# A segment softmax over sorted edges: carries applied to whole rows, or to the ends of a partition only

## The reference, cut to what matters

```
alpha = leaky_relu(s_src[row] + s_dst[col], negative_slope=0.2)      # (200000, 4)
seg_max = segment_max(alpha, row)
m = maximum(seg_max, 0.0)
ex = exp(alpha - m[row])
seg_sum = segment_sum(ex, row)
deg = segment_sum(ones, row)
denom = seg_sum + (E - deg)[:, None] * exp(-m)
alpha_n = ex / denom[row]
out = segment_sum(alpha_n[:, :, None] * h[col], col)                 # then + bias, residual
```

## Time and profile before

| | |
|---|---|
| median of three runs | 5434.14 us |
| span of the profiled execution | 5435.2 us |
| instructions | 98,961 |
| busy: PE, DVE, ACT, POOL | 4092.1, 3597.3, 3044.1, 3260.0 us |
| mean granted TensorE clock | 0.905 of full speed |

### The profile page before, as it was taken

The page is one execution under the profiler, slowest core; times in us unless marked ns, Lnnn a source line. Parts: engine busy times, 40 slices in busy tenths (PEclk is TensorE's granted clock), DMA queues, the critical chain, the costliest instruction groups (busy, mean ns, idle before and its releaser), DMA issues. The chain is left out here.

```text
span 5435.2 us, 98961 instructions
## 1 busy us (share of the span) xinstructions
PE 4092.1 (75%) x22798; PEld 3403.2 (63%) x22799; DVE 3597.3 (66%) x8070; ACT 3044.1 (56%) x4591; POOL 3260.0 (60%) x3487
## 2 busy tenths in 40 slices
PE   5778777777777777700699987777777777777778
PEld 5766666666666666500699965666666666666666
DVE  8945444444444444429999986777777777777776
ACT  5555555555555455401677756666666666666665
POOL 2357777777777777740000005777777777777774
PEclk9988888888888888855899999999999999999999
DMA  8865555555555554495200036666656565666655
GB/s 312 325 198 149 140 141 137 138 140 141 140 137 140 141 140 138 149 88 16 58 0 0 0 94 170 146 144 147 146 145 146 144 147 144 147 144 147 146 145 135
DMA packets 1212202, 734.52 MB, mean 135 GB/s; under 512 B 929642, under 2 KB 1031204, under 8 KB 1205388
## 3 DMA queue, kind: packets, MB, share of 16 engines
q1 hardware_dynamic: 862700, 336.19, 30.8%
q0 software_dynamic: 131424, 275.52, 17.3%
q10 hardware_dynamic: 218048, 122.49, 7.6%
HBM read 562.32 MB, written 165.09 MB: 134 GB/s over the span
## 5 line engine op out<-in xcount | busy, mean ns | idle before, releaser
L1059 POOL DMA_INDIRECT g_q<-q_d,g_aux x1660 | 1573.0, 948 | 1407.4 <-DMA pw<-g_q 901.7
L577 POOL DMA_INDIRECT rec_d<-rec,place x1568 | 1542.1, 984 | 503.2 <-issue 475.9
L1366 PE MATMUL g_hp<-pw,g_mix 128*128 x3328 | 876.0, 386 | 305.9 <-ACT g_mix L1263 300.6
L690 PE MATMUL lk<-tab_sd,low 128*128 128x196 f32 x3136 | 1065.5, 427 | 0.0
L1377 PE MATMUL g_ap<-g_hid,g_oh 128*128 128x256 f32 x3328 | 881.0, 387 | 140.2 <-DVE agg L1169 135.4
L626 DVE TENSOR_REDUCE rank<-equal 128x4 f32<-128x512 bf16 x392 | 260.6, 684 | 1024.9 <-ACT equal L554 1012.8
L1283 ACT ACTIVATE g_hid<-g_q 128x512 f32<-128x512 f32 x832 | 524.0, 630 | 713.6 <-DVE g_q L1155 698.4
L1366 PEld LDWEIGHTS g_hp<-pw,g_mix 128*128 128x128 f32 x3328 | 616.1, 190 | 463.7 <-issue 388.2
L1155 DVE TENSOR_TENSOR g_q<-g_hp,g_q 128x512 f32<-128x512 f32 x832 | 573.6, 689 | 477.3 <-DMA g_q<-q_d,g_aux 353.7
L687 PE MATMUL lk<-mask,hx 122*128 122x245 bf16 x1568 | 482.9, 308 | 430.6 <-ACT low L543 430.6
L554 ACT ACTIVATE equal<-rk,minus_two 128x512 bf16<-128x512 f32 x392 | 259.5, 685 | 967.5 <-DMA rec_d<-rec,place 561.3
(11 more groups left out here) (231 smaller groups left out, 5064.4 us busy)
## 6 DMA issues: line engine op xcount, KB each, us to landing
low_row<-rows_d SPq DMA_DIRECT2D x392, 256.0 KB
rec_d<-pad ACTq DMA_DIRECT2D x49, 1152.0 KB, 4.2
g_ea<-rec_d SPq DMA_DIRECT2D x208, 256.0 KB, 4.4
rec<-in_ea ACTq DMA_DIRECT2D x196, 256.0 KB
hx_row<-rows_d SPq DMA_DIRECT2D x392, 98.0 KB
g_lrow<-low_row_d SPq DMA_DIRECT2D x208, 128.0 KB, 4.3
g_q<-q_d,g_aux POOLq DMA_INDIRECT x1660, 2.9
rec_d<-rec,place POOLq DMA_INDIRECT x1568
```

The source lines that it names most:

```text
L577: pool.indirect_dma_start(rec_d, bass.IndirectOffsetOnAxis(ap=place[0:n, at, j:j + 1], axis=0), rec[0:n, at, j, :], None).then_inc(s_sc[at ...
L690: mm = pe.matmul(to[:, NB:LK], low[:, par, 1, slots], tab_sd[:, :, :].rearrange("p h a -> p (h a)"), start=False, stop=True, skip_group_ch ...
L1059: pool.indirect_dma_start(qg[:, par, j, :], None, q_d, bass.IndirectOffsetOnAxis(ap=aux[:, par, j, F_IDX - F_LOW:REC - F_LOW].bitcast(I32) ...
L1366: mm = pe.matmul(hp[u][:, k * HID:(k + 1) * HID], mix[:, par, 2 * u + k, :], pw[:, bass.ds(b[k], 1), :].rearrange("p o f -> p (o f)"), sta ...
```

## The change

Pieces are no longer joined in every slot. The scores have only the maximum of their own piece subtracted (`al - sc` right after the first `spread`), and the exponentials and sums are those of the piece. What was exchanged across partitions is joined in small tiles (`whole`): `peak` and `piece` hold, for the row's last and its first piece and four heads, the piece's own value and that of the whole run. The sums of the end pieces are scaled by `fall` = exp(own maximum - whole maximum) before they are exchanged. At the end ScalarE takes logarithms: of the piece sums in every slot (`line`), and of own and whole sums in the small tile `piece`. The difference of the small logarithms, less the difference of the maxima, is added to `line` in the slots of the first run (with `from_first`) and of the last run (with `to_last`); `one_run` keeps it from being added twice where a row holds one run alone. The weight is exp(`al` - `line`), by ScalarE.

```
+piece = sb("piece", [P, 2, 2, HEADS], F32, ctx)
+peak = sb("peak", [P, 2, 2, HEADS], F32, ctx)
+fall = sb("fall", [P, 2, HEADS], F32, ctx)
+one_run = sb("one_run", [P, 1], F32, ctx)
+tiny = sb("tiny", [P, 1], F32, ctx)
...
         act.activation(high_dst[:, at], fld[:, at, DHIGH], ACT.Copy).then_inc(s_ld, 1)
     for h in range(HEADS):
         act.wait_ge(s_mr, h + 1)
+        act.activation(line[h], al[:, h, :], ACT.Exp)
+        act.activation(sc[:, h, :], sc[:, h, :], ACT.Exp, scale=-1.0).then_inc(s_exp, 1)
+    act.wait_ge(s_mr, HEADS + 1)
+    act.activation(fall[:, :, :], peak[:, 1, :, :], ACT.Exp).then_inc(s_exp, 1)
+    for h in range(HEADS):
+        act.wait_ge(s_dn, h + 1)
+        act.activation(line[h], sc[:, h, :], ACT.Ln, bias=tiny[:, 0:1]).then_inc(s_ln, 1)
+    act.wait_ge(s_dn, HEADS + 1)
+    act.activation(piece[:, :, :, :], piece[:, :, :, :], ACT.Ln, bias=tiny[:, 0:1]).then_inc(s_ln, 1)
+    for h in range(HEADS):
+        act.wait_ge(s_fin, h + 1)
         act.activation(al[:, h, :], al[:, h, :], ACT.Exp)
-        act.activation(sc[:, h, :], sc[:, h, :], ACT.Exp, scale=-1.0).then_inc(s_exp, 1)
-    for pair in ((0, 1), (2, 3)):
-        for h in pair:
-            act.wait_ge(s_dn, h + 1)
-            act.activation(line[h], sc[:, h, :], ACT.Ln).then_inc(s_ln, 1)
-        for h in pair:
-            act.wait_ge(s_ln, h + 1)
-            act.activation(line[h], line[h], ACT.Exp, scale=-1.0).then_inc(s_r0, 1)
 @block.vector
 def _(v):
     link = Chain(v, s_ch)
+    v.memset(tiny[:, :], 1e-30)
     v.memset(fwd[:, S:S + 1], 0.0)
     v.memset(flagT[:, :, :], 0.0)
     v.memset(carT[:, :, :], 0.0).then_inc(s_e0, 1)
...
-    def carried(k, outs, op, both):
+    def carried(k, both):
...
-        for o, h in zip(outs, range(HEADS)):
-            ins = v.scalar_tensor_tensor(out=o, in0=from_first[:, :], scalar=car[:, 0, h:h + 1], in1=o,
-                                         op0=ALU.mult, op1=op)
-        link(ins)
-
-    def later(h, o, op):
-        return v.scalar_tensor_tensor(out=o, in0=to_last[:, :], scalar=car[:, 1, h:h + 1], in1=o, op0=ALU.mult, op1=op)
+    def whole(to, own, op):
+        v.scalar_tensor_tensor(out=to[:, 0, :], in0=car[:, 0, :], scalar=from_first[:, S - 1:S], in1=own[:, 0, :],
+                               op0=ALU.mult, op1=op)
+        link(v.scalar_tensor_tensor(out=to[:, 1, :], in0=car[:, 0, :], scalar=from_first[:, 0:1], in1=own[:, 1, :],
+                                    op0=ALU.mult, op1=op))
+        v.tensor_tensor(to[:, 0, :], to[:, 0, :], car[:, 1, :], op)
+        link(v.scalar_tensor_tensor(out=to[:, 1, :], in0=car[:, 1, :], scalar=to_last[:, 0:1], in1=to[:, 1, :],
+                                    op0=ALU.mult, op1=op))
...
+    v.tensor_scalar(one_run[:, :], from_first[:, S - 1:S], -1.0, 1.0, ALU.mult, ALU.add)
+    carried(0, False)
+    for h in range(HEADS):
+        ins = v.scalar_tensor_tensor(out=al[:, h, :], in0=from_first[:, :], scalar=car[:, 0, h:h + 1], in1=al[:, h, :],
+                                     op0=ALU.mult, op1=ALU.add)
+    link(ins)
...
-    def spread():
...
+    def spread(h):
+        return v.tensor_tensor_scan(sc[:, h, ::-1], next_no_head[:, ::-1], hd[:, ::-1, h], 0.0, ALU.mult, ALU.max)
+    for h in range(HEADS):
+        ins = spread(h)
+    link(ins)
+    v.tensor_copy(peak[:, 0, 0, :], hd[:, S - 1, 0:HEADS])
+    link(v.tensor_copy(peak[:, 0, 1, :], sc[:, :, 0]))
+    v.tensor_copy(ends[:, :, :], peak[:, 0, :, :]).then_inc(s_endr, 1)
     link(v.tensor_copy(low_in[:, :], fld[:, :, LOW]))
+    v.wait_ge(s_ld, CH)
+    for h in range(HEADS):
+        v.tensor_tensor(al[:, h, :], al[:, h, :], sc[:, h, :], ALU.subtract).then_inc(s_mr, 1)
+    link(v.tensor_scalar(low_out[:, :], low_in[:, :], BLK - 1, None, ALU.bitwise_and))
     exchange(1, ALU.max, True)
-    link(v.tensor_scalar(low_out[:, :], low_in[:, :], BLK - 1, None, ALU.bitwise_and))
-    carried(1, [sc[:, h, :] for h in range(HEADS)], ALU.max, True)
-    for h in range(HEADS):
-        link(later(h, sc[:, h, :], ALU.max))
-        v.tensor_tensor(al[:, h, :], al[:, h, :], sc[:, h, :], ALU.subtract).then_inc(s_mr, 1)
     v.tensor_copy(lowrow[:, :], low_out[:, :]).then_inc(s_lr, 1)
+    carried(1, True)
+    whole(peak[:, 1, :, :], peak[:, 0, :, :], ALU.max)
+    v.tensor_tensor(peak[:, 1, :, :], peak[:, 0, :, :], peak[:, 1, :, :], ALU.subtract).then_inc(s_mr, 1)
...
-        link(v.tensor_tensor(sc[:, h, :], sc[:, h, :], al[:, h, :], ALU.add))
+        link(v.tensor_tensor(sc[:, h, :], sc[:, h, :], line[h], ALU.add))
...
-    spread()
+    for h in range(HEADS):
+        spread(h).then_inc(s_dn, 1)
+    v.wait_ge(s_dn, HEADS)
+    v.tensor_copy(piece[:, 0, 0, :], hd[:, S - 1, 0:HEADS])
+    link(v.tensor_copy(piece[:, 0, 1, :], sc[:, :, 0]))
+    v.wait_ge(s_exp, HEADS + 1)
+    link(v.tensor_tensor(piece[:, 1, :, :], piece[:, 0, :, :], fall[:, :, :], ALU.mult))
+    v.tensor_copy(ends[:, :, :], piece[:, 1, :, :]).then_inc(s_endr, 1)
     exchange(2, ALU.add, True)
-    carried(2, [sc[:, h, :] for h in range(HEADS)], ALU.add, True)
+    carried(2, True)
+    whole(piece[:, 1, :, :], piece[:, 1, :, :], ALU.add)
+    v.engine_nop().then_inc(s_dn, 1)
+    v.wait_ge(s_ln, HEADS + 1)
+    link(v.tensor_tensor(piece[:, 0, :, :], piece[:, 1, :, :], piece[:, 0, :, :], ALU.subtract))
+    link(v.tensor_tensor(piece[:, 0, :, :], piece[:, 0, :, :], peak[:, 1, :, :], ALU.subtract))
+    link(v.tensor_scalar(piece[:, 0, 0, :], piece[:, 0, 0, :], one_run[:, 0:1], None, ALU.mult))
     for h in range(HEADS):
-        later(h, sc[:, h, :], ALU.add).then_inc(s_dn, 1)
-    v.wait_ge(s_ld, CH)
-    for h in range(HEADS):
-        v.wait_ge(s_r0, h + 1)
-        v.wait_ge(s_dn, h + 1)
-        link(v.tensor_tensor(line[HEADS], sc[:, h, :], line[h], ALU.mult))
-        link(v.scalar_tensor_tensor(out=sc[:, h, :], in0=line[HEADS], scalar=2.0, in1=line[h],
-                                    op0=ALU.subtract, op1=ALU.mult))
-        link(v.scalar_tensor_tensor(out=al[:, h, :], in0=al[:, h, :], scalar=-1.0, in1=sc[:, h, :],
-                                    op0=ALU.mult, op1=ALU.mult))
+        link(v.scalar_tensor_tensor(out=line[h], in0=from_first[:, :], scalar=piece[:, 0, 1, h:h + 1], in1=line[h],
+                                    op0=ALU.mult, op1=ALU.add))
+        link(v.scalar_tensor_tensor(out=line[h], in0=to_last[:, :], scalar=piece[:, 0, 0, h:h + 1], in1=line[h],
+                                    op0=ALU.mult, op1=ALU.add))
+        v.tensor_tensor(al[:, h, :], al[:, h, :], line[h], ALU.subtract).then_inc(s_fin, 1)
```

More of the change, by code:

```diff
@@ L745, in build @@
                 s_mr, s_exp = sem("max_taken"), sem("exp_ready")
-                s_dn, s_ln, s_r0 = sem("denominator_ready"), sem("log_ready"), sem("first_reciprocal_ready")
+                s_dn, s_ln, s_fin = sem("sums_spread"), sem("log_ready"), sem("log_weight_ready")
                 s_lr, s_ls, s_ld = sem("lowrow_ready"), sem("lowrow_stored"), sem("dst_digits_ready")
@@ L883, in _ @@
                     link(v.memset(to_last[:, S - 1:S], 1.0))
-                    rows = [al[:, h, :] for h in range(HEADS)]
-                    carried(0, rows, ALU.add, False)
+                    v.tensor_scalar(one_run[:, :], from_first[:, S - 1:S], -1.0, 1.0, ALU.mult, ALU.add)
[4 more added lines that the diff above has]
+                    link(ins)
                     for k in range(CH):
@@ L920, in _ @@
                         link(v.tensor_tensor(sc[:, h, :], sc[:, h, :], rest[:, :], ALU.mult))
-                        link(v.tensor_tensor(sc[:, h, :], sc[:, h, :], al[:, h, :], ALU.add))
+                        link(v.tensor_tensor(sc[:, h, :], sc[:, h, :], line[h], ALU.add))
                         ins = v.tensor_tensor_scan(hd[:, :, h], no_head, sc[:, h, :], 0.0, ALU.mult, ALU.add)
                     link(ins)
-                    spread()
-                    exchange(2, ALU.add, True)
```

## The result

The changed kernel takes 5405.74 us, the median of four runs (5404.22 to 5406.91), against 5434.32 us for the kernel before (four runs, 5433.72 to 5435.36): 28.6 us less, a ratio of 0.995 with a 95% interval of 0.9938 to 0.9962. The forecast was 5407.3 us and 26.8 us less.

What follows compares the result with a forecast made beforehand. VectorE was taken to bound the softmax stage: 54.58 us removed less 27.8 added gives 26.8, so 5434.14 - 26.8 = 5407.3 us. The stated range was 5404.5 to 5412.0, with the forecast given 0.89.

Steps and rivals of the forecast that it cites:

- The path: Softmax stage: VectorE alone sets its end, busy 125.2 of 128.5 us; a gain there reaches the kernel's end whole.
- the signs: Expected in the profile: second `spread` about 14.5 us earlier, last loop near 2576.4, weigh loop near 2601.8 at its old pace.
- What was removed: VectorE's softmax stage: sixteen long joins, the 0.89 us wait for reciprocals and twelve last-loop instructions, together 54.58 us.
- every microsecond off VectorE moves the barrier by one: Softmax stage, 2499.51 to 2627.98 us: VectorE time saved moves the barrier equally, as long as ScalarE does not become last.
- What was added: Softmax stage: new last loop 23.16, final exponential 1.63, small instructions 2.6 and round trip 0.4, together 27.8 us.
- The last loop: VectorE's end of the softmax stage: two linked instructions and one subtraction per head, 23.16 us, so no gain by itself.
- The tail: After VectorE's last subtraction: 0.04 us for ScalarE to notice and 1.59 for one exponential, 1.63 us.
- The round trip for the small logarithm: Before the last loop: VectorE waits for ScalarE's logarithm of 16 columns, 0.4 us, cheap end 0.2, dear end 1.0.
- The small instructions: Sixteen added on VectorE, ten linked at 0.20 and six at 0.08 or 0.10: 2.6 us, between 1.3 and 5.4.
- rival 1: End of softmax stage: ScalarE sets the end, four exponentials piling up behind VectorE, 6.0 us more, 5413.3; chance 0.05.
- rival 2: Weigh loop or gather stage: the gain is given back and the time stays near 5434; chance 0.03.
- rival 3: Loop bodies: moved code makes a loop fetch its body each turn, slower, 5716 at the dear side; chance 0.02.

Runs made afterwards that it cites:

- experiment 2: Kernel before without the sixteen joins over 1664 slots, 1 added in the logarithm: first spread scan to weigh loop 103.80 us, 25.2 less; median 5407.76 us.
- experiment 1: Changed kernel run again unaltered, twice: median 5411.69 us against 5436.55 for the kernel before, and on another chip 5401.31 against 5430.26.
- experiment 3: Kernel before with only the last step changed to exponentials of a difference of logarithms, long joins kept: median 5421.59 us against 5436.55.
- experiment 10: Kernel before with eight small memsets added to VectorE's program where it waits for a DMA: median 5430.96 us against 5430.26.
- experiment 4: Changed kernel without the eight long additions of the last loop: first spread scan to weigh loop 86.29 us, 15.9 less than changed; median 5394.02 us.
- experiments 7 and 8: Changed kernel with GpSimd subtracting `line` from `al`: median 5413.98 us; with GpSimd also multiplying by `rest`: 5419.12 us; kernel before 5435.71.

## Why the prediction was right

**The path.** The prediction held that VectorE's work sets the length of the stage, and that a microsecond at the barrier is worth a microsecond at the end. Both hold: the stretch fell by 26.84 us and the weigh loop kept its 578.53 us, to 0.02, in every kernel here. Counted from the first scan, the signs came where they were forecast: second `spread` 14.51 us earlier (14.5), last loop from 2572.07, which is 2576.58 on the clock of the kernel before (2576.4), weigh loop at 2601.69 (2601.8). The gather stage moves by 3.6 us, with no relation to the length of the stage ahead of it.

**What was removed.** 54.58 us, read from starts, was right as a sum for this change. It would have been wrong for the joins alone: experiment 2 shows that 5.4 of them covered ScalarE's logarithms and exponentials. So the prediction's rule that every microsecond off VectorE moves the barrier by one, as long as ScalarE does not become the last, is too strong: VectorE can also come to wait for ScalarE within the stage. In the changed kernel the logarithms have another cover, the scans of the second spread, as the prediction had it (last scan ends about 2566.7, last logarithm 2568.4, the small one asked for at 2571.06).

**What was added.** The last loop: 23.16 us by the sum; 2572.07 to 2593.37 + 1.89 = 2595.26 is 23.19. The tail: 1.63 forecast, 1.62 measured. The round trip for the small logarithm: 0.4 forecast; 0.42 from the end of the last small instruction, 2570.98, to 2571.40. The small instructions were sized too low: one `whole` takes 0.72 us, not 0.6, since an instruction of this size with a scalar read per partition takes 0.22 and not 0.17. With the `piece` steps they come to about 0.3 us more than the 2.6. The barrier made that good: the weigh loop begins 0.30 us after ScalarE's last exponential, where it began 0.55 after VectorE's last instruction. So the total, 26.84 for the stretch less 0.10 for `one_run` ahead of it (76.15 us against 76.05 from VectorE's first reduction over the node terms to the spread), meets 26.8 with two errors of 0.3 us that cancel, which is luck.

**The time.** 5405.74 lies 1.6 us under the forecast. No term of the sum explains that; experiment 1 shows the same kernel at 24.9 and 28.9 us under before. The prediction took the spread of three runs (0.8 us) for the noise of the kernel. Between sets of runs it is several times that: the same changed kernel has medians of 5405.74, 5411.69 and 5401.31 us, and the last, which is of another chip than the second, lies outside the stated range of 5404.5 to 5412.0. The gain of the stretch is shown; that the absolute time fell into so narrow a range is in part luck.

**The rivals.** ScalarE as the end (rival 1) did not come, with 4.2 us to spare a head; experiment 3 shows what it looks like where it does, at a cost of 0.2 us; the 6.0 us that the prediction gave it were seen in no run. A gain given back (rival 2) fails by the unchanged weigh loop and the gather stage. Moved code (rival 3) fails by the changed kernel itself, whose weigh and gather stages take 578.53 and 2075.9 us with ten blocks brought in as before, and by experiment 10: eight rows in VectorE's program change nothing there. That no position could do harm is not shown.

## What to carry to other kernels

Where a value must be joined across a boundary, join the few numbers at the boundary and carry the difference into the last pass over the data, in a form (a logarithm) in which it is an addition. That pass is not free: the additions still cost 15.9 us here (experiment 4). Before counting an instruction's time as a gain, ask what it covers on another engine: eight joins of 15.1 us were worth 9.7 alone. Fill the busiest engine's own waits with its own work before handing work to GpSimd: the four subtractions begun in VectorE's waits gained some 1.8 us, the same four on GpSimd lost 5.9.

## What the hardware showed that was not expected

While GpSimd ran subtractions and products of two tensors in SBUF, VectorE's instructions took longer by nearly whole ones of it: scans of 3.6 us took up to 7.06, a subtraction of 1.89 took 5.41, a copy of four columns 3.48 and `low_out`, with a single input tensor, 4.53 in place of 1.02 (experiments 7 and 8), while GpSimd's own went from 3.7 to as much as 7.0. The Trainium skill says so in SBUF — State Buffer, section SBUF: two separate sides: the port pair that the two engines share is an exclusive lock held for a whole instruction, which a VectorE instruction takes if it has two inputs in SBUF or runs in a mode that uses both ports. The traces agree that the two take turns; which mode the copy and `low_out` ran in, no run here shows. A bias read per partition made ScalarE's logarithm 1.68 us where the one with a constant took 1.59; the Trainium skill, in ScalarE: Activation LUTs, section What ACT_TABLE_LOAD costs, gives about 0.093 us for such an operand, and the difference of 0.09 agrees.
